# Two half-width maxima instead of one, and a wait of its own for the second head's matmul

## What is computed

```
q = layernorm(q) ; k = layernorm(k)              # per head, width 64
dots = einsum('bghqd,bgkd->bghqk', qg, k) * scale
attn = softmax(dots, axis=-1)
out  = einsum('bghqk,bgkd->bghqd', attn, v)
x    = x + out @ Wout
```

## Time and profile before

| | before |
|---|---|
| time, median of 3 runs | 841.31 us (840.61 to 843.43) |
| the profiled execution, span from first to last instruction | 838.9 us |
| PE busy | 810.6 us, 97% |
| DVE busy | 630.8 us, 75% |
| POOL busy | 587.2 us, 70% |
| ACT busy | 473.1 us, 56% |
| mean granted clock of PE | 0.998 |

### The profile page before, as it was taken

The page is one execution under the profiler, slowest core; times in us unless marked ns, Lnnn a source line. Parts: engine busy times, 40 slices in busy tenths (PEclk is TensorE's granted clock), DMA queues, the critical chain, the costliest instruction groups (busy, mean ns, idle before and its releaser), DMA issues.

```text
span 838.9 us, 13787 instructions
## 1 busy us (share of the span) xinstructions
PE 810.6 (97%) x5002; PEld 464.7 (55%) x5002; DVE 630.8 (75%) x1041; ACT 473.1 (56%) x849; POOL 587.2 (70%) x385
## 2 busy tenths in 40 slices
PE   6998999999999999999899999999999999999998
PEld 5664454444445444467544444454444444887687
DVE  6997888777778777366877788777777777677773
ACT  3865555555555655768655555555565556654622
POOL 3766668878877887946558888678888877355840
PEclk9999999999999999999999999999999999999999
DMA  6000000000000000000000000000000002200001
GB/s 179 1 2 1 1 1 2 1 1 1 2 1 1 2 1 1 1 1 2 1 1 1 1 1 1 1 1 2 1 1 1 2 1 52 45 10 2 1 1 51
DMA packets 49741, 8.00 MB, mean 10 GB/s; under 512 B 42502, under 2 KB 48266, under 8 KB 49674
## 3 DMA queue, kind: packets, MB, share of 16 engines
q1 hardware_dynamic: 48810, 6.99, 5.3%
q10 hardware_dynamic: 864, 0.13, 0.1%
HBM read 5.92 MB, written 1.05 MB: 8 GB/s over the span
## 4 chain that ended last, share of the span: by engine, by line
PE 80%; DVE 11%; issue 3%; ACT 2%; POOL 2%; DMA 1%; SPq 1%; DVEq 0%; POOLq 0%; ACTq 0%
PE psum L707 26%; PE psum L692 19%; PE psum L672 12%; PE psum L722 4%; DVE part L1236 4%; PE psum L735 3%; PE psum L1811 2%; PE psum L560 2%; PE psum L1838 1%; PE psum L562 1%; PE psum L561 1%; PE psum L1868 1%; DVE space L1252 1%; PE psum L1800 1%; PE psum L653 1%
## 5 line engine op out<-in xcount | busy, mean ns | idle before, releaser
L529 POOL TENSOR_TENSOR space<-space 128x1024 f32<-128x1024 f32 x160 | 380.4, 2378 | 23.7 <-ACT space L956 5.6
L1236 DVE TENSOR_REDUCE part<-psum 128x2 f32<-128x1024 f32 x256 | 313.2, 1224 | 110.6 <-PE psum L672 107.8
L956 ACT ACTIVATE space<-psum 128x512 f32<-128x512 f32 x512 | 264.5, 602 | 144.8 <-PE psum L692 121.5
L707 PE MATMUL psum<-space,vb 128*64 128x512 f32 x1024 | 247.5, 605 | 2.1 <-ACT space L956 2.1
L534 POOL TENSOR_TENSOR space<-space 128x1024 f32<-128x1024 f32 x30 | 71.5, 2385 | 100.3 <-DVE space L1252 100.3
L672 PE MATMUL psum<-kh,qh 64*128 64x512 f32 x512 | 127.4, 494 | 5.8 <-DVE part L1236 4.7
L707 PEld LDWEIGHTS psum<-space,vb 128*64 128x64 f32 x1024 | 62.5, 136 | 108.2 <-issue 71.7
L672 PEld LDWEIGHTS psum<-kh,qh 64*128 64x128 f32 x512 | 47.6, 183 | 132.2 <-DVE part L1236 99.3
L692 PE MATMUL psum<-qh,kh 64*128 64x512 f32 x512 | 103.3, 396 | 0.0
L692 PE MATMUL psum<-ql,kh 64*128 64x512 f32 x512 | 102.0, 390 | 0.0
L692 PE MATMUL psum<-qh,kl 64*128 64x512 f32 x512 | 101.9, 390 | 0.0
(11 more groups left out here) (249 smaller groups left out, 1034.0 us busy)
## 6 DMA issues: line engine op xcount, KB each, us to landing
ql<-nmx SPq DMA_DIRECT2D x256, 0.5 KB, 2.0
wproj<-in_L_ffn_W SPq DMA_DIRECT2D x4, 256.0 KB, 2.9
out<-x SPq DMA_DIRECT2D x3, 256.0 KB, 2.1
x<-in_L_attn_x SPq DMA_DIRECT2D x2, 256.0 KB, 4.4
wproj<-in_L_attn_Wq SPq DMA_DIRECT2D x1, 512.0 KB, 6.6
x<-in_L_attn_x SPq DMA_DIRECT2D x1, 512.0 KB, 7.5
wout<-in_L_attn_Wout SPq DMA_DIRECT2D x1, 512.0 KB, 7.1
w1s<-in_L_ffn_W SPq DMA_DIRECT2D x2, 256.0 KB, 3.1
```

The costliest lines, as they stand in the source:

```text
L529: pool.tensor_tensor(to, pt[0] if u == 1 else to, pt[u], ALU.add)\
L707: last = pe.matmul(outp[rows(h), :], vb[:, place(m)[1], kt, :], pt[kt][:, h, :], start=(kt == 0), stop=(kt == TILES - 1))
L956: act.activation(pt[kt][:, h, :], key_scores[kt % 2][h], ACT.Exp).then_inc(exp_made, 1)
L1236: dve.tensor_reduce(to[:, half, :], scores.rearrange("p (h k) -> p h k", h=2), AX_X, ALU.max, negate=True)\
```

## The change

For the first unit of each phase, DVE takes the maximum in two reductions of 512 columns, one for each head's bank: the first counts `part_made`, the second a new semaphore, `second_made`. On PE the second unit's head 0 waits for `part_made`, as before, and its head 1 now waits for `second_made`. The second unit's maximum stays one reduction, and the next phase's first unit waits for it alone. The joining reduction waits for `second_made` too. The arithmetic is the same.

```diff
+        second_made = sem("second_made")
...
                 for h in range(2):
+                    if h and k % 2:
+                        pe.wait_ge(second_made, 4 * n + k // 2 + 1)
                     last = pe.matmul(scores[:, h * 512:(h + 1) * 512],
...
-                dve.tensor_reduce(to[:, half, :], scores.rearrange("p (h k) -> p h k", h=2), AX_X, ALU.max, negate=True)\
-                   .then_inc(part_made, 1)
                 if half:
+                    dve.tensor_reduce(to[:, half, :], scores.rearrange("p (h k) -> p h k", h=2), AX_X, ALU.max, negate=True)\
+                       .then_inc(part_made, 1)
+                else:
+                    dve.tensor_reduce(to[:, 0, 0:1], scores[:, 0:512], AX_X, ALU.max, negate=True).then_inc(part_made, 1)
+                    dve.tensor_reduce(to[:, 0, 1:2], scores[:, 512:1024], AX_X, ALU.max, negate=True).then_inc(second_made, 1)
+                if half:
+                    dve.wait_ge(second_made, 4 * n + pair + 1)
```

## The result

| | before | after |
|---|---|---|
| time, median of the runs | 842.13 us (840.61 to 843.43, 4 runs) | 849.58 us (848.34 to 852.14, 4 runs) |
| the profiled execution, span | 838.9 us | 847.6 us |
| its own time | not given | 849.66 us |
| PE busy | 810.6 us, 97% | 821.1 us, 97% |
| DVE busy | 630.8 us, 75% | 635.9 us, 75% |

The ratio of after to before is 1.0093, 95% interval 1.0072 to 1.0113. The change made the kernel slower, by 7.4 us between the medians; the forecast was 848.4 us, 7.1 us above the 841.31 us that three runs of the kernel before had given; with the fourth their median is 842.13 us. The changed kernel was timed a second time, beside the experiments of the last group: 849.46 us, ratio 1.0086 (1.0072 to 1.0099).

The account below looks back on a forecast made before the run. PE, busy 97% of the span, was taken to bound the kernel; 6.4 us from 106 phases and 0.7 us from 12 early units, 7.1 us on the 841.3 us median, gave 848.4 us, range 844.5 to 853.0.

Parts of the forecast that it names:

- What bounds the loop: Second unit's wait for DVE's maximum, 106 phases: 0.09 us late plus 0.11 us for weights not loaded ahead, 21 us.
- the early parts: Units in `produce`, where the second waits for the first's maximum: 12 in all, each 0.06 us later, 0.7 us.
- The pair of reductions: DVE, first unit's maximum: two reductions of 512 columns take 1.28 us instead of 1.22, 0.06 us more.
- The rival of two reductions that do not overlap: DVE's two reductions run one after the other: 0.14 us in 118 places, 17.0 us, 858.3 us; chance 7%.
- Head 0: PE, second unit: waits for the first half alone, so its wait is gone and it starts 0.09 us earlier.
- Head 1 to the values: PE, second unit: from head 1's start to the values stays 0.43 us, the upper bound; 0.32 us the lower.
- The rival by which head 0's early start would shorten this: PE, head 1 to values: 0.32 us instead of 0.43, 4.6 us won, 836.7 us; chance 6%.
- No absorption: Opposed case: values' loads wait for exponentials and absorb the 0.06 us; only 0.7 us left, 842.0 us; chance 7%.
- The sum: Whole kernel: 106 x 0.06 = 6.4 us plus 12 x 0.06 = 0.7 us, 7.1 us slower.
- phases 6 to 10: Values lie between first and second unit there, so the added 0.06 us is covered.
- DVE's load: 128 more reductions on DVE, 7.7 us, lying in the 110.6 us it idles waiting for PE.

Follow-up runs that it names:

- the experiments of the last group: Against the kernel before: first unit's maximum split, PE untouched, 849.32 us; second unit's head 0 waiting for `second_made`, then `part_made`, 850.0 us; the changed kernel again, 849.46 us.
- half a maximum: Kernel before, with the first unit's maximum taken over only 256 of the 512 columns of each bank, in one reduction for both heads: 824.37 us, ratio 0.9795.
- The split with PE as before: Kernel before, with the first unit's maximum in two reductions, the second counting `part_made`, and PE's code untouched: 849.32 us, ratio 1.0089.
- The split of the second unit: Kernel before, with the second unit's maximum made in two reductions instead of the first's, and no new wait: 843.87 us, ratio 1.0015.
- ACT's copy: Kernel before; from phase 11 ACT copies head 1's bank of the first unit into SBUF, releasing head 1; DVE reduces bank 0, then the copy: 828.59 us.
- the first experiment: Changed kernel, with both heads of the second unit waiting for `part_made` and then `second_made`: 857.96 us, ratio to before 1.0194.
- the run with four reductions: Changed kernel, with the first unit's maximum in four reductions of 256 columns, head 0 released after two, head 1 after four: 864.13 us, ratio 1.0261.

## Why the prediction was right

- **What bounds the loop.** The second unit was said to be 0.09 us late and its weights not loaded ahead, 0.20 us a phase and 21 us in all. With half a maximum a phase wins 0.18 us, so the reading of the earlier trace rows was right to 0.02 us. The sum of 21 us was too large: the stretches fell by 14.8 us, because two phases grew by 4.0 us when the others got shorter. (The other 3.4 of the 18 us lie in the early parts, which the 21 us did not count.)
- **The pair of reductions, 0.06 us.** From the earlier trace rows 1.28 us was read, and it is 1.29 us. The rival of two reductions that do not overlap, 858.3 us, needed 1.37. It has fallen: L1244 starts 0.61 us after L1243 did, whose row lasts 0.69. The Trainium skill, page "VectorE: DVE Perf Modes", section "The DRAIN you can't avoid", was that rival's rule; the trace disagrees with it for two reductions without a wait between them, and fits the same section's remark that an instruction that isn't held starts earlier.
- **Head 0.** Its load was to start without a wait before 227.1 on the scale of the earlier trace rows, 1.5 us after the first unit; it starts 1.50 us after. The start of its matmul, 1.72 us after the first unit, is the 227.32 that was estimated for a unit without a wait. The split with PE as before shows that this gain does not get past head 1.
- **Head 1 to the values.** Of the two ends, 0.43 and 0.32 us, the upper one was taken, and it is 0.42 us. The rival by which head 0's early start would shorten this to under 0.37, 836.7 us, has fallen with it: head 1's load starts 0.06 us after its release, however early head 0's weights are there. The Trainium skill, page "TensorE: Matmul & The Clock Gate", section "Part 3: Packing small matmuls", says that a load for another row group, or into the background weight buffer, goes ahead of matmuls in flight. The trace shows head 0's load going ahead, at 229.00 beside a pair of matmuls of both heads, so also beside a matmul on its own rows; head 1's load, which waits, does not go ahead.
- **No absorption.** The values have moved by as much as head 1. In the changed kernel's waits, from 93.6 to 336.8 us, 150 of the 0.27 us ahead of the values' loads are put down to nothing, where the earlier trace rows gave 52 to the exponentials and 104 to nothing; their number and length are the same, which speaks against waits for ACT. That nothing was absorbed is shown by the two stretches, which grew by 6.1 us. The rows:

```profile
PEld psum L710 <- issue: 40.8, 150, 0.3
...
PEld psum L675 <- DVE part L1244: 11.2, 53, 0.4
```

  53 waits for L1244, one in each phase of the stretch and 0.21 us each, are the wait that the change left on head 1.
- **The sum.** 6.4 us were forecast for 106 phases, and the stretches grew by 3.2 + 2.9 = 6.1 us. For the early parts 0.7 us were forecast and 1.0 us came: the first 12 units of a batch grew by 0.40 and 0.43 us, about 0.07 us for each pair and not 0.06 (in the unit shown, the step from head 1 to the projection behind it takes 50.22 - 49.78 = 0.44 us where it took 0.42), and phases 6 to 10, where the shift was said to be covered, by 0.09 and 0.08 us. Together that is 7.1 us, as forecast; that the two misses of 0.3 us cancel is luck. The profiled spans differ by 8.7 us, of which the end of the program has 1.7; the medians, with 7.4 us, are the better measure.
- **DVE's load.** It was costed at nothing beyond the 0.06 us, since DVE idled 110.6 us ahead of these reductions. The split of the second unit, with the same load, took 0.6 us more in the two stretches.

What is still open: why the part behind the last unit varies by 2.7 us from profile to profile.

## What to carry to other kernels

Before a wait is split in two, look at what stands behind the later half: an engine that works in order takes up the gain of the first half at the next instruction that waits for the last, and what stays is the price of the split, here 0.06 us for every instruction more. What pays is to let the last part end earlier, for instance by giving half of the work to an engine that idles at that moment, as ACT's copy did here (ratio 0.9834). Where an instruction waits for two semaphores, put the one that ends last where the instruction itself carries it, and look in the trace which of them it is; here the one written first in the code was carried, and the one written last became the instruction ahead.

## What was not expected of the hardware

**The order of two waits on a weight load.** A wait that became an instruction of its own cost about 0.10 us each time it was the last to end (0.58 for 0.48 us from the reduction to the values), and nothing that could be told from noise where it had ended before: 857.96 against 850.0 us for the same waits. Part of it is that the two heads' loads come one after the other behind it: the first matmul starts 0.03 us after the first load, while the runs without it show both at the same time.

**A small operation on DVE that ended only with POOL's.** In the version with ACT's copy the longest phase starts at 171.93 and lasts 8.62 us. Timeline, DVE, POOL and PE:

```profile
173.10 1.94 DVE L1163 TENSOR_SCALAR st<-mv 128x8 f32<-128x8 f32 x1
```

```profile
165.05 9.95 POOL L540 TENSOR_TENSOR space<-space 128x1024 f32<-128x1024 f32 x4
```

```profile
171.93 0.51 PE L685 MATMUL psum<-kh,qh 64*128 64x512 f32 x2
...
175.68 0.50 PE L685 MATMUL psum<-kh,qh 64*128 64x512 f32 x2 [1.85 <-DVE part L1267]
176.11 3.35 PE L720 MATMUL psum<-space,vb 128*64 128x512 f32 x8
```

An operation over 8 columns takes 1.94 us and ends at 175.04; POOL's additions end at 175.00. The maximum behind it is late by that much, and PE waits 1.85 us for it. In the kernel before, the same operation of the same phase takes 0.26 us:

```profile
175.49 0.26 DVE L1136 TENSOR_SCALAR st<-mv 128x8 f32<-128x8 f32 x1
```

```profile
165.77 9.96 POOL L529 TENSOR_TENSOR space<-space 128x1024 f32<-128x1024 f32 x4
```

It too ends just after POOL's, 175.75 and 175.73; it had merely started later. So the faster loop brought this operation to a time at which POOL was busy for 1.9 us more, and it took 1.7 us longer. In other runs it falls where POOL is idle; in the first experiment (timeline, DVE) POOL's last addition had ended at 178.88:

```profile
179.06 0.17 DVE L1139 TENSOR_SCALAR st<-mv 128x8 f32<-128x8 f32 x1
```

So it does in the run with four reductions, 0.17 us too, while in the run with half a maximum it takes 1.82 us in batch 0 and 2.13 us in batch 1 and ends 0.03 us after POOL's each time. The Trainium skill, page "SBUF — State Buffer", section "Who interferes with whom", says that DVE and GpSimd share a pair of ports, that a `tensor_scalar` can be among the operations that take it, and that the one that issues second stands still until the first is done. These rows agree; that it is the ports, no run here shows.

**The values at the lower clock.** The values of that phase take 3.35 us and not 1.94, because the granted clock fell (busy time by stretch, columns as in the earlier trace rows):

```profile
176.49:179.90 3.41, 3.41 (x15) 1.39 (x13) 2.26 (x4) 0.00 (x0) 0.86 (x1) 0.50 0.04 5
```

It is 0.50 there, the lower level of 1.2 GHz, and 1.00 before (171.9 to 176) and after (180.55 to 182). PE had just idled for 1.85 us. In batch 1 the same operation takes 1.98 us, PE idles 1.90 us, the clock stays at 1.00 and the values take 1.94 us; that phase is 6.97 us long. In the run with half a maximum it is batch 1 that has the fall (0.50 from 512.50 us for 3.4 us, after 1.86 us of idling; the values take 3.61 us). So such an idle does not always bring the clock down, and what decides it no run here shows.
